# Moving a per-channel bias, a normalization and a residual shift between engines in a four-layer transformer kernel

## The chip, the cores and the metric

The kernel runs on one core of a Trainium2 chip. The metric is the device time of one execution in microseconds (us). The core has five engines that work side by side: TensorE (PE, with its weight loads as PEld), VectorE (DVE), ScalarE (ACT), GpSimd (POOL) and SyncE (SP, which only issues DMAs here). Each has its own queue of instructions, in order; between engines there are semaphores.

## The reference

32 sequences of 256 tokens with 128 channels go through four layers, each an attention-like and a feed-forward part with pre-normalization and a residual. The change touches three places.

The end of layer 0's attention-like part (a gated long convolution):

```
u, v, g = split(xn @ in_w + in_b)
y   = the state-space scan of silu(conv(u))
out = (y * sigmoid(g) + silu(v)) @ out_w + out_b
x   = x + out
```

Layer 3's mixer, a scan over time, where x is the normalized residual:

```
shifted = x moved one token later, a zero in front
inp = mix * x + (1.0 - mix) * shifted
h   = relu(inp @ W_in.T + b_in)
state = state * decay + h_t                            # over the 256 tokens
out = states @ W_out.T + b_out;   x = x + out
```

The very end: layer 3's feed-forward holds an attention, a mixture of 8 experts and a last normalization with gain `g2` and shift `ln2_b`; its result is added to the residual, so the shift can be added to the residual at any earlier time.

## The kernel before, in words

The residual `x_res` lies in SBUF for the whole kernel as 64 tiles of 128 tokens x 128 channels. A stage of this kind is a block in which each engine runs its own program over 16 units of 4 tiles (512 tokens). Stages are separated by barriers, and between them `stats` turns the collected `bn_stats` into mean and 1/deviation. A helper `staggered(engine, units, slots, (lag, work), ...)` writes a software pipeline: in step s it does, in the order listed, each piece of work for unit s - lag; the middle of it is a hardware loop. `sig.now(n, k)` is a wait for the k-th count of unit n, `sig.last(n, k)` for that of unit n-1, `sig.ago(n, k, m)` for that of unit n-m. `link` makes DVE wait for its own instruction.

Second stage of layer 0 ("c" in the names). Per step DVE does: normalize unit s (4 `tensor_scalar` of 128x128, helper line 411), add the projected output of unit s-3 to the residual (line 803) and take its `bn_stats` (line 345), then for unit s-1 and each of two channel blocks three 128x512 operations: `sv = (ps_v + bias) * sv` (line 790, one source in PSUM), `sg = sg * yT` (line 792) and `sv = sv + sg` (line 796), both with two sources in SBUF. PE projects unit s-1 (lines 831 and 832, into one PSUM buffer per block), turns unit s, projects unit s-2 out (line 841). ACT does the sigmoids of unit s-1 (lines 859, 861), moves the turned unit s out of PSUM (852), then scales the residual of unit s-1 (line 869, signal `c_grown`). POOL adds `out_b` to the residual, one 128x512 `tensor_tensor` per unit with both sources in SBUF (line 816); before it, POOL waits for `c_grown` of unit n and, while there is a unit n+2, for the normalization of unit n+2.

Mixer stage of layer 3 ("s"). ACT normalizes (line 2880, 4 activations per unit, three buffers `s_nrm`), PE turns, ACT copies `(1 - mix)` times the turned unit to `s_old` (line 2887), DVE mixes in one operation that reads the other part from PSUM (line 2815), PE projects, ACT applies the relu (2893), DVE scans (line 2822, two per unit), PE projects out (2861), DVE adds to the residual (2829) and takes the statistics. DVE's order in a step is add (lag 5), mix (lag 1), scan (lag 3). POOL adds `b_out` (line 2840) as soon as a unit is normalized.

Second attention ("h3"). After each sequence's attention, DVE adds the result to `x2`, takes `bn_stats` of it, and adds `b2` (the last shift) to two tiles of `x_res` (line 2400, 128x256). Then the router, and `sorted_experts`: DVE computes places, POOL issues 64 indirect DMAs that scatter the rows (line 1634) while DVE computes four small results more (lines 1553 to 1559).

Of the kernel before, what the change touches and what calls it, by code (L numbers as in the profile page):

```python
# [12 lines left out]
ACT = mybir.ActivationFunctionType  # L13
# [161 lines left out]
def build(nc, x_in, pack_in, maskb_in, w0_in, w1_in, w3_in, out, ktab, ychan, q_stack, k_stack, ones_rows, v_ones,  # L175
          m_parts, xs1, xs3, ys):
    ctx = ExitStack()
    with ctx:
# [132 lines left out]
        s_in, s_pr, s_re, s_sc, s_o, s_x = (sig("s_mixed", 1), sig("s_proj", 1), sig("s_relu", 1),  # L311
# [438 lines left out]
        with ExitStack() as st:  # L750
# [12 lines left out]
            with pool.loop_block(NU) as block:  # L763
# [760 lines left out]
        def sorted_experts(tag, sel, weight, src, xs, w, w_in, f_dim, func, normed=None, rows=None):  # L1524
# [13 lines left out]
            with ExitStack() as st:  # L1538
# [723 lines left out]
        def attend(tag, causal, dst, w, buffers, load, shifted=None):  # L2262
# [15 lines left out]
            with ExitStack() as st:  # L2278
# [40 lines left out]
                with pool.loop_block(NB) as block:  # L2319
# [21 lines left out]
                    def _(dve):  # L2341
# [44 lines left out]
                        def step(b, u, r, first, turn, body, tail):  # L2386
# [399 lines left out]
        with ExitStack() as st:  # L2786
            S = 3
            nrm = [sb(f"s_nrm{j}", [P, UT, P], stack=st) for j in range(S)]
            old = [sb(f"s_old{j}", [P, 2, SEQ + 1], stack=st) for j in range(S)]
            shift = sb("s_shift", [P, NT], stack=st)  # L2790
# [5 lines left out]
            ps_t = bank("s_ps_t", st, S)  # L2796
            ps_h = bank("s_ps_h", st, 2)
            ps_o = bank("s_ps_o", st, S)
            with pool.loop_block(NU) as block:
                k_set = n_chain[0] + 4 + S  # L2800

                @block.vector
                def _(dve):
                    for j in range(S):
                        link(dve, dve.memset(old[j][:, :, :], 0.0))
                    link(dve, dve.scalar_tensor_tensor(shift[:, :], mean[:, :], -1.0, rstd[:, :], ALU.mult, ALU.mult))
                    link(dve, dve.memset(dec[:, :], 1.0))
                    link(dve, dve.tensor_scalar(dec[:, :], dec[:, :], c("decay"), None, ALU.mult))
                    link(dve, dve.tensor_scalar(omix[:, :], c("mix"), -1.0, 1.0, ALU.mult, ALU.add))

                    def mix(n, j, r):
# [3 lines left out]
                        dve.scalar_tensor_tensor(mixed[j][:, :, :], ps_t[:, j, :].rearrange("p (b t) -> p b t", b=2), c("mix"),  # L2815
                                                 old[j][:, :, 0:SEQ], ALU.mult, ALU.add).then_inc(s_in.sem, 1)
# [16 lines left out]
                    staggered(dve, NU, S, (5, added), (1, mix), (3, scan))  # L2833
# [12 lines left out]
                def _(pe):  # L2846
                    def turn(n, j, r):
                        turn_tiles(pe, fr_s.tps, ps_t[:, j, :], nrm[j], UT, fr_s.nrm.now(n, 1), s_in.ago(n, 1, S))

                    def project(n, j, r, h):  # L2850
                        pe.wait_ge(*s_in.now(n, 1))
                        pe.wait_ge(*s_re.ago(n, 1, 2))
                        pe.matmul(ps_h[:, h, :], c("win3"), mixed[j][:, :, :].rearrange("p b t -> p (b t)"),
# [11 lines left out]
                    for n in range(NU + 4):  # L2865
                        if 0 <= n - 2 < NU:
                            project(n - 2, (n - 2) % S, (n - 2) // S, (n - 2) % 2)
                        if n < NU:
                            turn(n, n % S, n // S)
                        if 0 <= n - 4:  # L2870
                            project_out(n - 4, (n - 4) % S, (n - 4) // S)
# [256 lines left out]
```

## Time and profile before

| | |
|---|---|
| time, median of 3 runs | 3247.86 us (3245.29 to 3249.93) |
| time of the profiled execution | 3245.29 us |
| its span in the profile | 3243.2 us |
| TensorE clock granted, mean | 0.91 of full speed |
| busy in the span | PE 2553.1 us (79%), DVE 2129.7 (66%), ACT 1631.4 (50%), POOL 764.2 (24%) |
| second stage of layer 0 | from 271 to 393.5 us |
| mixer stage of layer 3 | from 2274.8 to 2345.0 us |
| second attention | from about 2480 to 2911.8 us |
| scatter before the last experts | from 2980 to 3061.5 us |

Shares are averages over many stages with different limits. The kernel is a chain of stages with barriers, so a stage's length is what counts, and in it the engine that is busy without a gap. The 2.1 us between the profiled time and its span lie outside the instructions.

### The profile page before, as it was taken

The numbers are of one execution on the slowest core, as the hardware profiler recorded it, in microseconds if no ns is written. First come the engines' busy times: TensorE is split into PE (matmuls) and PEld (weight loads), VectorE is DVE, ScalarE is ACT, GpSimd is POOL, SyncE is SP. The second block draws the span as 40 slices with busy tenths as digits, with TensorE's granted clock in tenths as the row PEclk, the third lists the DMA queues.
The fourth block names the chain that finished last, engine by engine and source line by source line (L and its number), as shares of the span: only waits on it lengthen the run. The fifth ranks groups of instructions, "written<-read, shape, count | busy, mean of one in ns | idle before, by whom it ended". The sixth has DMA issues, their size and how long they took to land. (4 is left out here: it accounts for less than half of the span.)

```text
span 3243.2 us, 69838 instructions
## 1 busy us (share of the span) xinstructions
PE 2553.1 (79%) x20225; PEld 1822.0 (56%) x20225; DVE 2129.7 (66%) x4755; ACT 1631.4 (50%) x3623; POOL 764.2 (24%) x1097
## 2 busy tenths in 40 slices
PE   4657859989988786999459999997676999984191
PEld 2334543449877533999237777767443666653180
DVE  5967875237778633777756666657876888855086
ACT  1646513332254443667535666652553777764063
POOL 0000100000000176555432222200251222211670
PEclk7889979999999898999779999998888999997595
DMA  3095100111190211222594566500086566521133
GB/s 104 0 213 143 46 13 20 35 43 49 36 172 0 78 53 51 71 69 67 171 243 53 72 72 70 69 6 1 1 263 68 72 72 72 72 25 45 52 100 111
DMA packets 316152, 241.10 MB, mean 74 GB/s; under 512 B 27069, under 2 KB 297837, under 8 KB 315693
## 3 DMA queue, kind: packets, MB, share of 16 engines
q1 hardware_dynamic: 288248, 202.91, 31.6%
q0 software_dynamic: 19072, 28.28, 3.0%
q10 hardware_dynamic: 8704, 8.39, 0.9%
q8 instruction: 58, 0.95, 0.1%
q14 instruction: 70, 0.57, 0.1%
HBM read 139.83 MB, written 96.51 MB: 73 GB/s over the span
## 5 line engine op out<-in xcount | busy, mean ns | idle before, releaser
L2619 ACT ACTIVATE h_pt<-h_ps 128x384 f32<-128x384 f32 (+1 forms) x1024 | 543.5, 545 | 278.1 <-PE h_ps L2528 143.5
L2365 DVE TENSOR_REDUCE h_nm<-h_ps 128x4 f32<-128x1024 f32 (+1 forms) x448 | 539.2, 1218 | 153.9 <-PE h_ps L2499 62.3
L1900 POOL DMA_INDIRECT results<-e_y,e_ykey x208 | 217.0, 1043 | 162.6 <-DVE e_y L1889 143.5
L1857 DVE TENSOR_SCALAR e_wt<-w 128x1156 f32 (+1 forms) x208 | 141.2, 680 | 166.1 <-PEq L1626 87.7
L2547 PE MATMUL h_ps_o<-h_pt,h_vp 128*32 128x256 f32 (+1 forms) x4096 | 246.8, 358 | 1.3 <-ACT h_pt L2619 1.3
L1947 ACT ACTIVATE e_hid<-e_ps_h,e_wt 128x128 f32<-128x128 f32 x688 | 201.3, 369 | 13.4 <-PE e_ps_h L1921 8.8
L2533 PE MATMUL h_ps<-h_sq,h_sk 128*128 128x256 bf16 x1024 | 193.4, 275 | 9.2 <-ACT h_pt L2619 4.3
L1929 PE MATMUL e_ps_o<-e_wt,e_hid 128*128 128x128 f32 x1376 | 192.4, 279 | 4.8 <-DVE e_y L1889 4.8
L1921 PE MATMUL e_ps_h<-e_hT,e_wt 128*128 128x128 f32 x1376 | 195.1, 281 | 0.6 <-ACT e_hT L1942 0.3
L2470 PE MATMUL h_ps<-h_sk,h_sq 128*128 128x256 bf16 x1024 | 156.1, 276 | 42.6 <-DVE h_identb L2347 36.6
L1704 POOL DMA_INDIRECT sorted_rows<-e_row,e_pos x128 | 124.6, 974 | 256.2 <-DVE e_row L1682 218.3
L1921 PEld LDWEIGHTS e_ps_h<-e_hT,e_wt 128*128 128x128 f32 x1376 | 172.3, 194 | 9.0 <-issue 3.2
L1929 PEld LDWEIGHTS e_ps_o<-e_wt,e_hid 128*128 128x128 f32 x1376 | 170.7, 192 | 8.1 <-DVE e_y L1889 8.0
L1942 ACT ACTIVATE e_hT<-e_ps_t 128x128 f32<-128x128 f32 x208 | 57.6, 278 | 217.7 <-PE e_ps_t L1914 211.3
L2547 PEld LDWEIGHTS h_ps_o<-h_pt,h_vp 128*32 128x32 f32 x4096 | 106.8, 109 | 92.5 <-issue 36.7
L2414 POOL TENSOR_TENSOR h_mpart<-h_nm,h_zero 128x32 bf16<-128x32 f32 x64 | 15.0, 234 | 580.5 <-DVE h_nm L2365 580.5
L1914 PE MATMUL e_ps_t<-pack,e_xt 128*128 128x128 f32 x208 | 57.5, 278 | 110.2 <-DMA e_xt<-sorted_rows 110.0
L2525 PE MATMUL h_ps<-h_sq,h_sk 128*128 128x256 bf16 x512 | 140.4, 274 | 2.1 <-ACT h_pt L2619 1.7
L349 PE MATMUL stats_ps_d<-pack 128*128 128x384 f32 x136 | 65.9, 654 | 96.7 <-PEq L166 86.3
L2528 PE MATMUL h_ps<-h_mskb 128*128 128x256 bf16 x512 | 139.6, 273 | 0.0
L1223 DVE TENSOR_TENSOR x_hid<-x_gelu,x_ps_u 128x512 f32<-128x512 f32 x64 | 43.3, 686 | 142.3 <-ACT x_gelu L1208 142.3
L2470 PEld LDWEIGHTS h_ps<-h_sk,h_sq 128*128 128x128 bf16 x1024 | 99.7, 99 | 59.1 <-DVE h_identb L2347 36.8
(457 smaller groups left out, 6249.7 us busy)
## 6 DMA issues: line engine op xcount, KB each, us to landing
h_sk<-k_stack SPq DMA_DIRECT2D x192, 128.0 KB
q_stack<-p_parts SPq DMA_DIRECT2D x64, 256.0 KB, 3.0
h_sq<-q_stack SPq DMA_DIRECT2D x64, 256.0 KB
sorted_rows<-pad SPq DMA_DIRECT2D x26, 520.0 KB, 10.6
e_xt<-sorted_rows SPq DMA_DIRECT2D x104, 130.0 KB, 2.2
e_got<-results SPq DMA_DIRECT2D x24, 512.0 KB, 4.7
k_stack<-p_parts SPq DMA_DIRECT2D x32, 384.0 KB, 3.0
b_tz<-ktab SPq DMA_DIRECT2D x32, 256.0 KB, 7.1
```

The source lines that it names most:

```text
L1857: dve.tensor_scalar(wt[j % 4][:, :], w[:, :, :].rearrange("p e w -> p (e w)")[:, ds(at, wc)], 1.0, None, ALU.mult).then_inc(e_w.sem, 1)
L1900: gp.indirect_dma_start(ys[:, :], bass.IndirectOffsetOnAxis(ap=key[m // 4][:, m % 4:m % 4 + 1], axis=0), y[m][:, :], None).then_inc(return ...
L1921: pe.matmul(ps_h[:, k, 0:P], wt[j % 4][:, f * P:(f + 1) * P], hT[j % 4][:, :], start=True, stop=True).then_inc(e_h.sem, 1)
L1929: ins = pe.matmul(o, hid_t[m][:, f, :], wt[m][:, f_dim + f * D:f_dim + (f + 1) * D], start=(f == 0), stop=(f == nf - 1))
L1947: act.activation(hid_t[j % 4][:, f, :], ps_h[:, (j * nf + f) % 4, 0:P], func, bias=wt[j % 4][:, o_b1 + f:o_b1 + f + 1]).then_inc(e_a.sem, 1)
L2365: dve.tensor_reduce(to, got, AX, ALU.max, negate=True).then_inc(s["mx"].sem, 1)
L2470: ins = pe.matmul(ps_1[:, h % 4, q * SEQ:(q + 1) * SEQ], sq[u][:, h, q * P:(q + 1) * P], sk[u][:, h, :], start=True, stop=True)
L2525: pe.matmul(o[:, 0:SEQ], sk[u][:, hd, 0:P], sq[u][:, hd, :], start=True, stop=False, skip_group_check=True)
L2528: ins = pe.matmul(o.rearrange("p (t q) -> p t q", q=SEQ)[:, :, 0:P], mskb[:, 0:P], mskb[:, 2 * P:3 * P].unsqueeze(1).to_broadcast([P, 2, P ...
L2533: ins = pe.matmul(o[:, t * SEQ:(t + 1) * SEQ], sk[u][:, hd, t * P:(t + 1) * P], sq[u][:, hd, :], start=True, stop=True)
L2547: ins = pe.matmul(ps_o[32 * j:32 * (j + 1), q0:], vp[u % 2][:, t, head(HG * g + j), :], pt[g % 2][:, j, t * SEQ:(t + 1) * SEQ - q0], start ...
L2619: act.activation(pt[g % 2][:, j, :], ps_2[:, h % 2, 0:SW], ACT.Exp, scale=scale).then_inc(s["ex"].sem, 1)
```

## The change

Three things are rewritten.

1. Stage c: POOL no longer waits for the normalization of unit n+2 before it adds `out_b`, and its program becomes a `staggered` loop. PE's projection of a block waits until DVE has finished the previous unit's last operation on that block (`c_z`, line 796), where it waited for the first (`c_v`, line 790).
2. Stage s: the normalization goes from ACT to DVE (helper line 411) with one buffer `s_nrm` in place of three; ACT copies the turned unit unscaled to `s_hT`; the mix becomes two DVE operations, both from SBUF; PSUM buffers for the turned and the projected unit go from 3 and 2 to 1 each; DVE's order becomes normalize (lag 0), add (4), scan (2), mix (1).
3. The 32 adds of `b2` inside the second attention go, and one 128x8192 add stands behind DVE's small results in the scatter block.

```diff
@@ stage c, POOL
                         gp.wait_ge(*c_grown.now(n, 1))
-                        if not isinstance(n, int) or n + 2 < NU:
-                            gp.wait_ge(*fr_c.nrm.now(n + 2, 1))
...
-                    for n in range(NU):
-                        biased(n, n % S, n // S)
+                    staggered(gp, NU, S, (0, biased))
@@ stage c, PE
                         for b in range(CB):
-                            pe.wait_ge(*c_v.last(n, b + 1))
+                            pe.wait_ge(*c_z.last(n, b + 1))
@@ stage s, buffers
-            nrm = [sb(f"s_nrm{j}", [P, UT, P], stack=st) for j in range(S)]
-            old = [sb(f"s_old{j}", [P, 2, SEQ + 1], stack=st) for j in range(S)]
-            shift = sb("s_shift", [P, NT], stack=st)
+            nrm = sb("s_nrm", [P, UT, P], stack=st)
+            hT = [sb(f"s_hT{j}", [P, 2, SEQ + 1], stack=st) for j in range(S)]
...
-            ps_t = bank("s_ps_t", st, S)
-            ps_h = bank("s_ps_h", st, 2)
+            ps_t = bank("s_ps_t", st)
+            ps_h = bank("s_ps_h", st)
@@ stage s, DVE
+                    def normed(n, j, r):
+                        norm_tiles(dve, fr_s.nrm, nrm, x_res, n * UT, UT, rstd, fr_s.tps.last(n, 1))
...
-                        dve.scalar_tensor_tensor(mixed[j][:, :, :], ps_t[:, j, :].rearrange("p (b t) -> p b t", b=2), c("mix"),
-                                                 old[j][:, :, 0:SEQ], ALU.mult, ALU.add).then_inc(s_in.sem, 1)
+                        dve.tensor_scalar(mixed[j][:, :, :], hT[j][:, :, 0:SEQ], omix[:, :], None, ALU.mult
+                                          ).then_inc(s_in0.sem, 1)
+                        dve.wait_ge(*s_in0.now(n, 1))
+                        dve.scalar_tensor_tensor(mixed[j][:, :, :], hT[j][:, :, 1:], c("mix"), mixed[j][:, :, :],
+                                                 ALU.mult, ALU.add).then_inc(s_in.sem, 1)
...
-                    staggered(dve, NU, S, (5, added), (1, mix), (3, scan))
+                    staggered(dve, NU, S, (0, normed), (4, added), (2, scan), (1, mix))
@@ stage s, PE
-                    for n in range(NU + 4):
...
+                    staggered(pe, NU, S, (2, project), (0, turn), (3, project_out))
@@ stage s, ACT
-                    def normed(n, j, r):
...
-                        act.activation(old[j][:, :, 1:], ps_t[:, j, :].rearrange("p (b t) -> p b t", b=2), ACT.Copy,
-                                       scale=omix[:, :]).then_inc(fr_s.hT.sem, 1)
+                        act.activation(hT[j][:, :, 1:], ps_t[:, 0, :].rearrange("p (b t) -> p b t", b=2), ACT.Copy
+                                       ).then_inc(fr_s.hT.sem, 1)
...
-                    for n in range(NU + 3):
-                        for lag, work in ((3, positive), (0, normed), (1, older)):
+                    staggered(act, NU, S, (2, positive), (0, turned))
@@ second attention, DVE
-                                if shifted is not None:
-                                    x_last = x_res[:, ds((b - 1) * TPB, TPB), :]
-                                    dve.tensor_tensor(x_last, x_last, shifted.unsqueeze(1).to_broadcast([P, TPB, D]), ALU.add)
@@ scatter block, DVE
                             places(dve)
+                            beside(dve)
...
+                def residual_shifted(dve):
+                    link(dve, dve.tensor_tensor(x_res[:, :, :], x_res[:, :, :], c("b2").unsqueeze(1).to_broadcast([P, NT, D]),
+                                                ALU.add))
```

On PE at the start of stage c, the instructions stand as they did; what a projection (`c_ps_v`) waits for is another signal. `signal32` is DVE's `c_v`, `signal33` its `c_z`, `signal38` ACT's moved unit `c_hT`. Before:

```order
L420 MATMUL c_ps_t<-pack,c_nrm 128x128 x3
L831 MATMUL c_ps_v<-c_hT,pack 128x512 [waits signal32,signal38]
L832 MATMUL c_ps_g<-c_hT,pack 128x512
L831 MATMUL c_ps_v<-c_hT,pack 128x512 [waits signal32]
L420 MATMUL c_ps_t<-pack,c_nrm 128x128 [waits signal38,signal30]
```

Now:

```order
L420 MATMUL c_ps_t<-pack,c_nrm 128x128 x3
L828 MATMUL c_ps_v<-c_hT,pack 128x512 [waits signal33,signal38]
L829 MATMUL c_ps_g<-c_hT,pack 128x512
L828 MATMUL c_ps_v<-c_hT,pack 128x512 [waits signal33]
L420 MATMUL c_ps_t<-pack,c_nrm 128x128 [waits signal38,signal30]
```

Each pair of projections moved behind two more DVE operations of the unit ahead of it; the turning of the next unit stands behind them in PE's queue as it did.

On DVE at the start of stage s, from the memsets to the second scan (`s_mix` is the mixed input, `s_state` the scan's result, `s_rel` the relu's). Before:

```order
L2805 MEMSET s_old 128x514 x3
L2806 SCALAR_TENSOR_TENSOR s_shift<-mean,rstd 128x64
L2807 MEMSET s_dec 128x256
L2808 TENSOR_SCALAR s_dec<-s_dec,pack 128x256
L2809 TENSOR_SCALAR s_omix<-pack 128x1
L2815 SCALAR_TENSOR_TENSOR s_mix<-s_ps_t,pack,s_old 128x512 x3
L2822 SCALAR_TENSOR_TENSOR s_state<-s_dec,s_rel 128x256 x2
```

Now:

```order
L2799 MEMSET s_hT 128x514 x3
L2800 MEMSET s_dec 128x256
L2801 TENSOR_SCALAR s_dec<-s_dec,pack 128x256
L2802 TENSOR_SCALAR s_omix<-pack 128x1
L411 TENSOR_SCALAR s_nrm<-x_res,mean,rstd 128x128 x8
L2811 TENSOR_SCALAR s_mix<-s_hT,s_omix 128x512
L2814 SCALAR_TENSOR_TENSOR s_mix<-s_hT,pack,s_mix 128x512
L411 TENSOR_SCALAR s_nrm<-x_res,mean,rstd 128x128 x4
L2821 SCALAR_TENSOR_TENSOR s_state<-s_dec,s_rel 128x256 x2
```

Four small operations and a second mixing operation per unit came to DVE, and a unit is scanned one step after it is mixed, where two steps lay between.

On DVE in the scatter block, where `e_past` to `e_place` are the small results and the next block begins with the loads of `e_place`. Before:

```order
L1553 TENSOR_TENSOR e_past<-pack,e_tend 128x504
L1557 TENSOR_REDUCE e_placef<-e_past 128x72
L1558 TENSOR_SCALAR e_placef<-e_placef 128x72
L1559 CAST e_place<-e_placef 128x72
L1626 UNCONDITIONAL_BRANCH
```

Now:

```order
L1550 TENSOR_TENSOR e_past<-pack,e_tend 128x504
L1554 TENSOR_REDUCE e_placef<-e_past 128x72
L1555 TENSOR_SCALAR e_placef<-e_placef 128x72
L1556 CAST e_place<-e_placef 128x72
L2937 TENSOR_TENSOR x_res<-x_res,pack 128x8192
L1623 UNCONDITIONAL_BRANCH
```

The add of 64 tiles stands last in the block, behind everything that another engine needs from DVE there.

## Rows read from the trace of the kernel before

**Rows 1.** Windows: stretch, length, busy PE PEld DVE ACT POOL, PEclk, DMA share, GB/s.

```profile
292.00:330.00 38.00, 34.88 (x163) 20.53 (x162) 35.49 (x83) 29.37 (x54) 7.67 (x6) 1.00 0.25 81
2289.00:2327.00 38.00, 27.40 (x138) 19.05 (x138) 36.62 (x80) 27.82 (x61) 14.17 (x10) 0.91 0.00 1
2500.00:2910.00 410.00, 399.10 (x4161) 252.62 (x4160) 326.52 (x473) 298.33 (x602) 96.67 (x261) 1.00 0.53 64
```

**Rows 2.** Timeline: start, us, engine, line, operation; DVE over one unit, second stage.

```profile
326.22 1.11 DVE L411 TENSOR_SCALAR c_nrm<-x_res,mean,rstd 128x128 f32 x4
327.24 0.68 DVE L803 TENSOR_TENSOR x_res<-x_res,c_ps_o 128x512 f32 x1
...
328.99 0.73 DVE L790 SCALAR_TENSOR_TENSOR c_sv<-c_ps_v,pack,c_sv 128x512 f32<-128x512 f32 x1
...
331.69 0.68 DVE L792 TENSOR_TENSOR c_sg<-c_sg,c_yT 128x512 f32<-128x512 f32 x1
332.48 0.69 DVE L796 TENSOR_TENSOR c_sv<-c_sv,c_sg 128x512 f32<-128x512 f32 x1
333.21 1.11 DVE L411 TENSOR_SCALAR c_nrm<-x_res,mean,rstd 128x128 f32 x4
```

**Rows 3.** Timeline: PE, ACT and POOL around the same unit.

```profile
324.96 1.13 PE L831 MATMUL c_ps_v<-c_hT,pack 128*128 128x512 f32 x2
...
326.98 0.69 ACT L859 ACTIVATE c_sv<-c_ps_v,pack 128x512 f32<-128x512 f32 x1 [0.70 <-PE c_ps_g L832]
...
327.47 1.28 POOL L816 TENSOR_TENSOR x_res<-x_res,spread 128x512 f32<-128x512 f32 x1 [5.70 <-DVE c_nrm L411]
...
328.85 1.64 ACT L869 ACTIVATE x_res<-x_res,c_sink,c_grow  x4
```

**Rows 4.** Timeline: DVE and POOL at the same stage's end, POOL not waiting for DVE.

```profile
378.82 0.69 DVE L796 TENSOR_TENSOR c_sv<-c_sv,c_sg 128x512 f32<-128x512 f32 x1
...
379.20 1.44 POOL L816 TENSOR_TENSOR x_res<-x_res,spread 128x512 f32<-128x512 f32 x1 [1.82 <-ACT x_res L869]
...
380.09 1.10 DVE L792 TENSOR_TENSOR c_sg<-c_sg,c_yT 128x512 f32<-128x512 f32 x1
```

**Rows 5.** Timeline: DVE and ACT in the scan stage.

```profile
2289.77 0.99 DVE L345 BATCH_NORM_STATS2 bn<-x_res  x4
...
2326.90 2.30 DVE L2822 TENSOR_TENSOR_SCAN s_state<-s_dec,s_rel 128x256 f32<-128x256 f32 x2
...
2329.81 0.87 DVE L345 BATCH_NORM_STATS2 bn<-x_res 128x6 f32<-128x128 f32 x4
...
2331.25 1.27 DVE L2822 TENSOR_TENSOR_SCAN s_state<-s_dec,s_rel 128x256 f32<-128x256 f32 x2
...
2332.55 0.69 ACT L2893 ACTIVATE s_rel<-s_ps_h,pack 128x512 f32<-128x512 f32 x1 [3.08 <-PE s_ps_h L2853]
```

**Rows 6.** Groups by line: names, shapes, count, busy us, mean ns, idle before.

```profile
L590 DVE TENSOR_SCALAR a_cv<-a_up,pack 128x512 f32<-128x512 f32 x32 | 15.9, 539 | 0.0
...
L1396 DVE TENSOR_SCALAR l_low<-l_qk 128x512 f32<-128x512 f32 x32 | 13.7, 427 | 1.1
```

**Rows 7.** Timeline: first and last work of the scan stage.

```profile
2274.75 1.65 ACT L2880 ACTIVATE s_nrm<-x_res,s_shift,rstd 128x128 f32<-128x128 f32 x4 [5.42 <-DVE s_omix L2809]
...
2344.11 0.87 DVE L345 BATCH_NORM_STATS2 bn<-x_res 128x6 f32<-128x128 f32 x4
```

**Rows 8.** Group and timeline: the add of b2, end of the second attention.

```profile
L2400 DVE TENSOR_TENSOR x_res<-x_res,pack 128x256 f32 (+1 forms) x32 | 13.0, 407 | 0.0
...
2911.36 0.41 DVE L2400 TENSOR_TENSOR x_res<-x_res,pack 128x256 f32<-128x256 f32 x1
```

**Rows 9.** Timeline: DVE beside POOL's indirect DMAs, and DVE after the last scatter.

```profile
1126.09 0.97 POOL L1704 DMA_INDIRECT sorted_rows<-e_row,e_pos  x1 [0.30 <-issue]
1126.27 1.14 DVE L1553 TENSOR_TENSOR e_past<-pack,e_tend 128x952 f32<-128x952 f32 x1
...
3069.22 0.98 DVE L1857 TENSOR_SCALAR e_wt<-w 128x642 f32 x2 [87.74 <-PEq L1626]
```

More of the change, by code:

```diff
@@ L1519, in _, with sorted_experts @@
                     staggered(act, NB, S, (2, gated), (0, keep), (2, powers))
-        def sorted_experts(tag, sel, weight, src, xs, w, w_in, f_dim, func, normed=None, rows=None):
+        def sorted_experts(tag, sel, weight, src, xs, w, w_in, f_dim, func, normed=None, rows=None, beside=None):
             choices = len(sel)
@@ L2260, in build, with attend @@
         BLOCKS = GROUPS // 2
-        def attend(tag, causal, dst, w, buffers, load, shifted=None):
+        def attend(tag, causal, dst, w, buffers, load):
             s = attns[tag]
@@ L2804, in _ @@
                     for j in range(S):
-                        link(dve, dve.memset(old[j][:, :, :], 0.0))
-                    link(dve, dve.scalar_tensor_tensor(shift[:, :], mean[:, :], -1.0, rstd[:, :], ALU.mult, ALU.mult))
+                        link(dve, dve.memset(hT[j][:, :, :], 0.0))
                     link(dve, dve.memset(dec[:, :], 1.0))
@@ L2847, in turn, with project @@
                     def turn(n, j, r):
-                        turn_tiles(pe, fr_s.tps, ps_t[:, j, :], nrm[j], UT, fr_s.nrm.now(n, 1), s_in.ago(n, 1, S))
-                    def project(n, j, r, h):
+                        turn_tiles(pe, fr_s.tps, ps_t[:, 0, :], nrm, UT, fr_s.nrm.now(n, 1), fr_s.hT.last(n, 1))
+                    def project(n, j, r):
                         pe.wait_ge(*s_in.now(n, 1))
-                        pe.wait_ge(*s_re.ago(n, 1, 2))
-                        pe.matmul(ps_h[:, h, :], c("win3"), mixed[j][:, :, :].rearrange("p b t -> p (b t)"),
+                        pe.wait_ge(*s_re.last(n, 1))
+                        pe.matmul(ps_h[:, 0, :], c("win3"), mixed[j][:, :, :].rearrange("p b t -> p (b t)"),
                                   start=True, stop=True).then_inc(s_pr.sem, 1)
@@ L2875, in _, with turned @@
                     act.wait_ge(chained, k_set)
-                    def normed(n, j, r):
-                        act.wait_ge(*fr_s.tps.ago(n, 1, S))
-                        for t in range(UT):
-                            ins = act.activation(nrm[j][:, t, :], x_res[:, n * UT + t, :], ACT.Identity,
-                                                 scale=rstd[:, n * UT + t:n * UT + t + 1], bias=shift[:, n * UT + t:n * UT + t + 1])
-                        ins.then_inc(fr_s.nrm.sem, 1)
-                    def older(n, j, r):
+                    def turned(n, j, r):
                         act.wait_ge(*fr_s.tps.now(n, 1))
                         act.wait_ge(*s_in.ago(n, 1, S))
-                        act.activation(old[j][:, :, 1:], ps_t[:, j, :].rearrange("p (b t) -> p b t", b=2), ACT.Copy,
-                                       scale=omix[:, :]).then_inc(fr_s.hT.sem, 1)
+                        act.activation(hT[j][:, :, 1:], ps_t[:, 0, :].rearrange("p (b t) -> p b t", b=2), ACT.Copy
+                                       ).then_inc(fr_s.hT.sem, 1)
                     def positive(n, j, r):
@@ L2892, in positive @@
                         act.wait_ge(*s_sc.ago(n, 2, S))
-                        act.activation(rel[j][:, :, :], ps_h[:, n % 2, :].rearrange("p (b t) -> p b t", b=2), ACT.Relu,
+                        act.activation(rel[j][:, :, :], ps_h[:, 0, :].rearrange("p (b t) -> p b t", b=2), ACT.Relu,
                                        bias=c("bin3")).then_inc(s_re.sem, 1)
-                    for n in range(NU + 3):
-                        for lag, work in ((3, positive), (0, normed), (1, older)):
-                            if 0 <= n - lag < NU:
-                                work(n - lag, (n - lag) % S, (n - lag) // S)
+                    staggered(act, NU, S, (2, positive), (0, turned))
         stats(x_res)
@@ L2907, in build @@
                                       bv=every_row("bv3")), heads_in, load_heads, keep=(x2, every_row("bo3")))
[L2908 removed]
+            attend("h3", False, x2, dict(o=c("wo3")), heads_in, load_heads)
             stats(x2)
@@ L2951, in build @@
                 stl.close()
-                sorted_experts("e3", (chosen[:, :, :],), (gp[:, :],), x2, xs3, w, w3_in, F3, ACT.Relu, rows=x2_rows)
+                def residual_shifted(dve):
+                    link(dve, dve.tensor_tensor(x_res[:, :, :], x_res[:, :, :], c("b2").unsqueeze(1).to_broadcast([P, NT, D]),
+                                                ALU.add))
+                sorted_experts("e3", (chosen[:, :, :],), (gp[:, :],), x2, xs3, w, w3_in, F3, ACT.Relu, rows=x2_rows,
+                               beside=residual_shifted)
             collect("e3", 1, x2)
```

11 lines of the change are left out of this document (2 added, 9 removed).

## The prediction

> **What bounds the kernel now.** I read the stage windows first, then the timeline of one unit in each changed stage, then the edges of the stages. The windows [rows 1] give the limit of each: in 38 us of stage c DVE is busy for 35.49, in 38 us of stage s for 36.62, and in 410 us of the second attention PE is busy for 399.10 and DVE only for 326.52. So the two first stages last as long as DVE's queue, and what the change adds there is paid in full; the attention lasts as long as PE's queue, and what it takes from DVE there is not. The unit in stage c [rows 2] shows it again: normalizations start at 326.22 and 333.21, 6.99 apart, and DVE's records follow each other all the way.
>
> **Stage c.** DVE's own operations stay. What changes is when POOL adds `out_b`. Before, POOL waits for the normalization and runs at 327.47 [rows 3], beside DVE's add that reads PSUM, which keeps its 0.68 us [rows 2]; nobody loses. Without the wait POOL starts when ACT has scaled the residual. What then happens is seen where the kernel before has no unit n+2 to wait for [rows 4]: POOL starts at 379.20 while DVE's SBUF-SBUF add (378.82 to 379.51) still runs, takes 1.44 in place of 1.28 and ends at 380.64, 1.13 after that add; the next DVE operation with two SBUF sources starts at 380.09 and takes 1.10 in place of 0.68, ending 0.55 after POOL. So POOL's add and such a DVE operation exclude each other. The Trainium skill (SBUF — State Buffer, "Who interferes with whom") has the rule: a VectorE instruction with two SBUF inputs contends with a GpSimd instruction that reads SBUF, and whoever is first holds the port for its whole instruction. By that rule every collision costs the later engine what is left of the earlier one's instruction, and the trace agrees, with its 0.42 us; were the port shared by halves, the loss would be half of the overlap, 0.28 for the 0.55 that line 792 spends beside POOL.
>
> Where does POOL land now? Offsets are from DVE's normalization at 326.22. PE may start block 1's projection only after the last operation of the unit before on that block, which ends at about 0.0 (333.17 for the next step), so at 0.1; before, it started at 324.96, that is -1.26. ACT's first sigmoid of that block comes 2.02 after PE's start, and ACT's scaling of the residual 1.87 after that sigmoid, behind a second sigmoid and the move of the turned unit (326.98 and 328.85, [rows 3]): 2.1 and 4.0. The scaling's 1.64 ends at 5.6, where it ended at 4.3. Nothing in DVE waits for this: the two sigmoids (0.69 each) are done by 3.5, and block 1's first DVE operation stands just ahead of line 792, at 4.8. POOL asks at 5.7 to 5.8. DVE's line 792 holds 5.47 to 6.15 [rows 2], so POOL's add ends 1.13 later, at 7.28, and line 796, which would start at 6.26, ends 0.55 after that at 7.83 in place of 6.95: +0.88. In units where ACT's scaling comes a little later, POOL finds line 796 in its place, ends at 8.1 and holds the next normalization: +1.1. I take 0.9 for 16 units, 14.4, less three stalls of about 0.42 that the kernel before already has at the stage's first and last units [rows 4], 1.3. PE's later start costs something in the first unit or two, when nothing is buffered; at most the two operations it now waits for, 0.69 + 0.69 [rows 2]; I take 1. Stage c: 14.4 - 1.3 + 1.0 = **+14.1**. Bounds: only one 0.42 per unit, as in [rows 4], makes +5.4; 1.1 each and 1.4 at the start make +17.7.
>
> **Stage s.** Before, ten units take from 2289.77 to 2329.81 [rows 5], 4.00 each. After, I add up DVE's queue per step. Normalization, add and statistics are the same sequence as in stage c, and the operation behind them starts 2.77 after the normalization (328.99 - 326.22, [rows 2]); I use that for the scans' start. Two scans take 1.27 [rows 5] and the next operation starts 0.09 before they end (as 327.24 against 326.22 + 1.11 in [rows 2]): 1.18. The mix is now two operations. No row has the first one, a 128x512 `tensor_scalar` with one pointer scalar: [rows 6] has 0.427 with none and 0.539 with two, so it lies between and I take 0.48. The second waits for it (0.10, as line 796 behind line 792: 332.48 - 332.37 in [rows 2]) and is priced as line 790, a `scalar_tensor_tensor` of that size, 0.73. Mix: 0.48 + 0.10 + 0.73 - 0.09 = 1.22. Step: 2.77 + 1.18 + 1.22 = **5.17**, against 4.00.
>
> Does anything make it longer? The scan needs the relu. It ends 2.0 us after the mix before it (2331.25 is the mix's end less 0.08, the relu ends at 2333.24, [rows 5]), and 2.77 of other DVE work lies between. At half clock two projections take about 1 us more, and the relu would end at 3.0: a wait of 0.2 in such a step. POOL's add starts 0.14 to 0.2 behind the normalization (327.47 against 327.33, [rows 2, 3]), so it lasts from 1.3 to 2.6, beside the add that reads PSUM and the statistics, and is out just before the scans at 2.77. Before, some scan pairs collided with it, 2.30 for 1.27 [rows 5]; that loss is inside the 4.00. If POOL's add lasted into the scans it would cost up to 1.0 per step.
>
> The new order has 12 full steps (4 to 15) in its loop: 12 x 5.17 = 62.0. The four filling steps run on latency: with one `s_nrm`, the second normalization waits until PE has turned the first; then mix, projection, relu and scan one after another. From DVE's records and PE at half clock I get 5.5 for steps 0 and 1, 5.3 for step 2 and 4.8 for step 3, 15.6. The four draining steps: 4.7 (add, statistics, a wait for the relu, scans, mix), 3.4, 1.75 and 1.75, 11.6. Start: 2274.75 less the small operation that is gone, 2274.4 [rows 7]. End: 2274.4 + 15.6 + 62.0 + 11.6 = 2363.6, against 2344.11 + 0.87 = 2344.98 [rows 7]. Stage s: **+18.6**. Bounds: +15 if the first mix is at 0.43, the fill at 14 and the drain at 10; +25 if the relu or POOL's add costs 0.5 in each full step. ACT loses 64 activations, which cost nothing and save nothing.
>
> **Second attention.** Gone are 32 adds of 0.407 [rows 8], 13.0 of DVE. They lie beside PE, whose idle time is 11 us of 410 [rows 1]. Only the last has nothing to hide it: it is the stage's last work, 2911.36 [rows 8]. **-0.4**; bounds 0 and -11.
>
> **Scatter block.** The new add has 8192 columns. [rows 9]: 952 columns take 1.14; with 512 in 0.69 [rows 2] a column costs 1.02 ns, so 8192 take 8.6 us. It is hidden: DVE is idle for 87.74 before its next block while POOL scatters [rows 9]. POOL's indirect DMAs must not be held by it; the one row of such a DVE operation beside them has POOL at its 0.97 and DVE at its 1.14 [rows 9]. **0**, at worst +8.6. The Trainium skill warns, in DMA: Bandwidth & Descriptors ("SWDGE vs HWDGE vs iDMA"), that GpSimd writes its descriptors through the SBUF access from which VectorE's 2-port modes lock it out; SBUF — State Buffer, "Who interferes with whom", adds that `tensor_tensor` takes only the read side and did not stall them. If the add locked POOL out, the block would be up to 8.6 longer, by the second sentence nothing; the one row that the trace has agrees with the second.
>
> **Sum.** 14.1 + 18.6 - 0.4 + 0 = +32.3. The profiled execution took 3245.29, so 3277.6; it is the fastest of the three runs, and on their median 3247.86 I get 3280.2. I predict **3280**.
>
> **Rivals.**
> - *The collision in stage c is cheap.* POOL's request falls just behind a DVE operation that reads PSUM, and each unit pays the 0.42 of [rows 4], stage c +5.4: 3271. For it: that is the only price seen in steady rows. Against: there PE's projection was 1.26 earlier.
> - *Both stages lose their margin.* In c 1.1 per unit, in s 0.5 per step from POOL's add or a half-clock PE: 17.7 + 25 - 0.4 = +42: 3290. For it: the margins in s are 0.1 to 0.2 us.
> - *The big add stops POOL's scatter,* +8.6: 3289. POOL's next indirect DMA would wait for DVE's whole instruction. Against it stands [rows 9]; for it, that this row covers 1.1 us and not 8.6.
> - *The attention was paced by DVE after all, and the kernel is not slower.* PE's ends are modelled, and its 399.10 busy of 410 [rows 1] may hide waits for maxima behind the adds. The removal must then shorten each of 32 sequences by 32.7 / 32 = 1.02 us, 2.5 times the operation removed, to bring the time to 3248 or less; from there the kernel is not slower. Taking just the operations' own 13.0 gives 3268. Against: DVE is idle for 83 of the 410 us there.
> - *The change doesn't do what it says* in c: POOL's wait gone moves nothing, since ACT's scaling comes as late as the normalization. Then c is +1 and the time 3267. Against: POOL asks at 5.8, and the old wait ended at 8.1 (6.99 + 1.11, [rows 2]).
>
> **Chances.** Forecast (3275 to 3286) 0.58; cheap collision 0.13; margins lost 0.12; scatter held 0.06; POOL unmoved 0.07; attention paced by DVE 0.04, of which half reaches no change. Range: 3266 to 3292; it leaves out the far ends of both sides. A measurement can tell about 0.2% from no change, 6.5 us: faster 0.01, same 0.02, slower 0.97.
>
> **What would show it.** In stage c: line 796 of block 1 (or the normalization behind it) at 1.5 us and more where it was 0.69, POOL's add starting inside DVE's line 792, and normalizations 7.9 apart. In s: starts of normalization 5.2 apart, no idle time on DVE in the full steps, scans at 1.27 a pair, the first mix at 0.48, the stage about 89 us long. In the attention the same length to a microsecond, with DVE 13 less busy. In the scatter block an add of 8.6 us and indirect DMAs at 0.97 throughout. I am wrong if the units of c stay 7.0 apart, if those of s come nearer to 4 than to 5, or if the attention gets shorter by more than 2 us.

## The result

The changed kernel takes 3276.06 us (median of 4 runs, 3275.61 to 3285.74), the kernel before beside it 3246.57 us (median of 4, 3245.17 to 3249.93): a ratio of 1.0096, 95% interval 1.0084 to 1.0108. It is slower by 0.96%; the forecast was 3280 in a range of 3266 to 3292, and "slower" had 0.97. The profiled execution of the changed kernel has a span of 3278.0 us against 3243.2, so the profiles have 34.8 us to explain, for which the prediction had 32.3.

The sum is near, but its parts are not all right. Each stage ends in a short stretch of statistics whose first record (line 361 of both kernels) cuts the span into stretches that can be compared:

| stretch | before us | after us | difference | predicted |
|---|---|---|---|---|
| start to the end of stage c | 393.75 | 403.55 | +9.8 | +14.1 |
| five unchanged stretches to the start of stage s | 1873.24 | 1872.87 | -0.4 | 0 |
| stage s | 78.30 | 98.46 | **+20.2** | +18.6 |
| projections and second attention | 566.78 | 564.95 | -1.8 | -0.4 |
| scatter block, experts, collection | 293.60 | 301.78 | **+8.2** | 0 |
| the rest | 37.55 | 36.39 | -1.2 | 0 |

The start holds an unrelated +1.0 (first statistics at 52.3 and 53.3) and -1.5 up to stage c's first normalization (271.11 and 270.61); from that normalization to its statistics stage c takes 122.64 before and 132.95 after, **+10.3**. Unchanged stretches differ by 1 us and more between executions (567.90 and 566.69, 108.80 and 109.77), so neither -1.8 nor -1.2 needs a cause.

The windows that answer to [rows 1] (same columns), the middle one over the longer stage s:

```profile
292.00:330.00 38.00, 29.88 (x140) 18.07 (x139) 35.82 (x73) 26.21 (x47) 6.76 (x6) 1.00 0.21 68
...
2284.00:2374.00 90.00, 55.40 (x224) 36.51 (x224) 80.22 (x206) 20.21 (x32) 20.38 (x16) 0.79 0.00 0
...
2529.00:2939.00 410.00, 398.65 (x4155) 252.12 (x4152) 318.45 (x442) 297.55 (x601) 91.69 (x261) 1.00 0.53 64
```

In stage c DVE is as full as before (35.82 of 38) with 73 instructions where it did 83: same busy share, less work. In the attention DVE lost 8 us of busy time in this window (the prediction's sign was 13) and PE did not change.

**Stage c after.** The timeline of DVE, ACT and POOL over one unit (start, duration, engine, line; in brackets the engine's idle time before it and what ended it):

```profile
339.46 1.10 DVE L411 TENSOR_SCALAR c_nrm<-x_res,mean,rstd 128x128 f32 x4
...
343.43 1.64 ACT L866 ACTIVATE x_res<-x_res,c_sink,c_grow  x4
...
344.96 0.68 DVE L792 TENSOR_TENSOR c_sg<-c_sg,c_yT 128x512 f32<-128x512 f32 x1
345.27 1.49 POOL L814 TENSOR_TENSOR x_res<-x_res,spread 128x512 f32 x1 [6.28 <-ACT x_res L866]
345.74 1.57 DVE L796 TENSOR_TENSOR c_sv<-c_sv,c_sg 128x512 f32<-128x512 f32 x1
...
347.23 1.10 DVE L411 TENSOR_SCALAR c_nrm<-x_res,mean,rstd 128x128 f32 x4
```

Read against [rows 2]: normalizations are 7.77 apart, not 6.99. ACT's scaling ends at 345.07, POOL starts 5.81 after the normalization, inside line 792 (344.96 to 345.64), and ends at 346.76; line 796 ends 0.55 later at 347.31, as the chain in the prediction had it, with 1.57 us where [rows 2] has 0.69. The groups of DVE in the stage (count, then busy us and mean ns of one) say what that comes to, the kernel after:

```profile
L796 DVE TENSOR_TENSOR c_sv<-c_sv,c_sg 128x512 f32<-128x512 f32 x32 | 32.9, 1027 | 3.3
...
L792 DVE TENSOR_TENSOR c_sg<-c_sg,c_yT 128x512 f32<-128x512 f32 x32 | 23.5, 734 | 0.0
L411 DVE TENSOR_SCALAR c_nrm<-x_res,mean,rstd 128x128 f32 (+1 forms) x64 | 18.8, 353 | 1.2 <-PE c_ps_t L420 1.2
```

and before:

```profile
L792 DVE TENSOR_TENSOR c_sg<-c_sg,c_yT 128x512 f32<-128x512 f32 x32 | 23.1, 723 | 0.0
L796 DVE TENSOR_TENSOR c_sv<-c_sv,c_sg 128x512 f32<-128x512 f32 x32 | 22.1, 692 | 3.3
L411 DVE TENSOR_SCALAR c_nrm<-x_res,mean,rstd 128x128 f32 (+1 forms) x64 | 17.8, 341 | 1.4 <-PE c_ps_t L420 1.2
```

The mean of 1027 hides two values, 0.69 and 1.57. That is 10.8 + 0.4 + 1.0 = 12.2 us more of DVE for the same work, some of it in the filling units, where DVE waits anyway. A line of 796 with a mean of 1027 ns and no wait in front of it is what this contention looks like in a profile: it is counted as busy time of the operation and never as idle time.

**Stage s after.** DVE, PE, ACT and POOL over one full step:

```profile
2326.49 1.11 DVE L411 TENSOR_SCALAR s_nrm<-x_res,mean,rstd 128x128 f32 x4
2326.71 2.07 PE L2852 MATMUL s_ps_h<-s_mix,pack 128*128 128x512 f32 x2 [2.52 <-DVE s_mix L2814]
2327.52 0.68 DVE L2828 TENSOR_TENSOR x_res<-x_res,s_ps_o 128x512 f32 x1
2327.80 1.26 POOL L2839 TENSOR_TENSOR x_res<-x_res,spread 128x512 f32 x1 [3.82 <-DVE s_nrm L411]
2328.34 0.98 DVE L345 BATCH_NORM_STATS2 bn<-x_res  x4
...
2328.91 0.69 ACT L2879 ACTIVATE s_rel<-s_ps_h,pack 128x512 f32<-128x512 f32 x1 [4.91 <-PE s_ps_h L2852]
...
2329.63 1.28 DVE L2821 TENSOR_TENSOR_SCAN s_state<-s_dec,s_rel 128x256 f32<-128x256 f32 x2 [0.30 <-ACT s_rel L2879]
...
2330.82 0.46 DVE L2811 TENSOR_SCALAR s_mix<-s_hT,s_omix 128x512 f32<-128x512 f32 x1
2331.32 0.75 DVE L2814 SCALAR_TENSOR_TENSOR s_mix<-s_hT,pack,s_mix 128x512 f32<-128x512 f32 x1
```

Every duration of the step's sum is there: scans at 1.28 a pair (none at 2.30 as in [rows 5]), the first mix at 0.46 (taken: 0.48), the second at 0.75 (0.73). The starts of the twelve full steps are 5.2 apart on average. This step is the longest of them, 5.55: PE's two projections took 2.07 where others take 1.12 (granted clock 0.50 of full speed from 2326.7 to 2328.8, 0.99 in the 5 us before), so the relu came late and the scans waited 0.30. The prediction had put 0.2 on that. In these full steps POOL's add meets no long record of DVE; in the filling ones it meets two, a normalization (four from 2285.91 take 1.45 for 1.11) and a second mix (1.64 at 2287.80 for 0.75).

**The scatter block after.** DVE and POOL:

```profile
3004.86 0.68 DVE L1550 TENSOR_TENSOR e_past<-pack,e_tend 128x504 f32<-128x504 f32 x1 [0.88 <-PEq L1571]
3005.15 1.30 POOL L1632 DMA_INDIRECT sorted_rows<-x,e_pos  x1 [90.94 <-PEq L1623]
...
3006.75 8.73 DVE L2937 TENSOR_TENSOR x_res<-x_res,pack 128x8192 f32<-128x8192 f32 x1
3006.76 0.99 POOL L1632 DMA_INDIRECT sorted_rows<-x,e_pos  x1 [0.30 <-issue]
3008.06 8.27 POOL L1632 DMA_INDIRECT sorted_rows<-x,e_pos  x1 [0.30 <-issue]
3016.63 0.97 POOL L1632 DMA_INDIRECT sorted_rows<-x,e_pos  x1 [0.30 <-issue]
```

One indirect DMA takes 8.27 us, from 3008.06 to 3016.33: it ends 0.85 after DVE's add (3015.48). The 64 scatters take 7.6 us longer, first start to last (80.4 before, 87.9 after). That is the rival with 0.06 in the prediction, and it came true. The two POOL rows above the long one matter too. The DMA that starts together with the add has 0.99 and is not stalled; the first one, which starts inside a 504-column `tensor_tensor`, has 1.30 (in the kernel before the first one starts 0.01 after that `tensor_tensor` has ended, and has 1.04).

### The profile page after: what moved, and what is told of

The parts are those of the page before. It is cut to its first block and busy times, and to the rows that moved or that the text cites. A ratio compares the mean times of both kernels' runs of the same rounds, so it can differ in the third digit from the quotient of the medians.

```text
span 3278.0 us, 70059 instructions
## 1 busy us (share of the span) xinstructions
PE 2556.2 (78%) x20225; PEld 1825.7 (56%) x20225; DVE 2164.3 (66%) x4803; ACT 1606.8 (49%) x3559; POOL 769.1 (23%) x1097
```

## The experiments

The kernel before ran at 3277, 3290 and 3245 us in the three sets of runs below: the level differs from set to set, mostly by the two expert stages (the stretch between the fourth and the fifth statistics took 541 us in the first profile, 539 in the last set and 557 to 567 in the two between, in kernels that leave it untouched). So a ratio is taken only against the kernel before of its own set, and stage lengths come from each run's own profile. Stages c and s are nearly free of that (c 121.7 to 123.6, the stretch of s 77.8 to 79.9, in all kernels that do not touch them). The five runs from PE's wait alone to POOL's later add in stage s are one execution each: they are read by the lengths of their stages and not by their total.

**The three parts alone.** First stage c, all its edits, on the kernel before (POOL's loop becomes a `staggered` one as well; not shown here):

```
-                        if not isinstance(n, int) or n + 2 < NU:
-                            gp.wait_ge(*fr_c.nrm.now(n + 2, 1))
-                            pe.wait_ge(*c_v.last(n, b + 1))
+                            pe.wait_ge(*c_z.last(n, b + 1))
```

> The kernel before with the edits of stage c alone: POOL's out_b add no longer waits for the normalization two units later, and PE's projection waits for the last add of the unit before on its block (c_z) instead of its first operation (c_v). Theory (the SBUF access is held for a whole instruction; POOL's add lands inside line 792 of block 1 and line 796 behind it waits): stage c +10.3 us as in the changed kernel (from the first normalization to the statistics 122.6 before, 133.0 after), twelve steady units at 7.9 instead of 7.0, line 796 of block 1 at 1.57; total +9 to +11. Rival (the collisions of stage c are an effect of the whole changed program, such as where its other stages leave the clock): stage c within 2 us of before.

Measured: ratio 1.0039 (1.0025 to 1.0053), +12.8 us by that ratio (9 to 11 were expected); stage c 132.87, +10.2; line 796 of block 1 at 1.57 to 1.61 in eleven consecutive units. As the theory has it, and independent of the other parts: from the second on, the normalizations are as far apart as in the changed kernel to 0.01 us.

The edits of stage s alone (all of that stage's part of the diff):

> The kernel before with the edits of stage s alone. Theory: DVE's queue sets the step, 5.2 us in twelve full steps; stage s (first normalization to the end of its last statistics) 90.5 in place of 70.2, total +19 to +21. Rival (part of the stage's loss in the changed kernel comes from a lower clock handed on by stage c or the tail): under +17.

Measured: ratio 1.0057 (1.0040 to 1.0074), +18.7 us, just under the 19 to 21 that were expected; the stretch of stage s 98.07 us, against 98.46 in the changed kernel and 78.30 before. The loss is there without the other parts. From the first normalization to the end of the last statistics it is 88.7 us, against 90.7 in the changed kernel and 70.2 before; the remaining 1.3 us or so of the stretch lie ahead of the first normalization, which comes 9.05 after the statistics' first record (7.49 in the changed kernel, and 9.31 in the next run, whose stage s is the old one).

The move of the `b2` adds alone (32 adds out of the attention, one beside the scatter):

> The kernel before with the adds of b2 moved alone: the 32 of the second attention gone, one 128x8192 add beside POOL's scatter. Theory (a tensor_tensor of two SBUF sources holds back POOL's indirect DMA for its whole length): one indirect DMA of about 8.3 us, the stretch from the attention's statistics to the last statistics 8 us longer, the attention 0.4 to 2 shorter; total +6 to +8. Rival (the 8 us of the changed kernel's scatter block come from elsewhere, such as slower transfers behind it): indirect DMAs at 0.97 and total -2 to 0.

Measured: ratio 1.0028 (1.0010 to 1.0046), +9 us, the expected 6 to 8 being well inside the interval. The profile of this kernel, DVE and POOL in the scatter block:

```profile
2998.80 8.76 DVE L2952 TENSOR_TENSOR x_res<-x_res,pack 128x8192 f32<-128x8192 f32 x1
2998.84 0.99 POOL L1635 DMA_INDIRECT sorted_rows<-x,e_pos  x1 [0.30 <-issue]
3000.13 8.27 POOL L1635 DMA_INDIRECT sorted_rows<-x,e_pos  x1 [0.30 <-issue]
3008.71 0.97 POOL L1635 DMA_INDIRECT sorted_rows<-x,e_pos  x1 [0.30 <-issue]
```

The same 8.27, the scatters again 87.6 from first to last. The attention's stretch took 564.87, inside the 562.5 to 568.6 of all kernels, with and without these adds: its gain cannot be told from nothing (seven kernels with the adds have a mean of 565.7, five without them 564.4).

The three ratios add up to +1.24%, with an uncertainty of about 0.28%, against +0.96% for the whole change: too coarse to show whether the parts are independent. The profiles' lengths are finer: 10.2 in stage c, 19.8 in the stretch of stage s and 7.3 in the scatters, 37.3 together, against 10.3, 20.2 and 7.6 in the changed kernel.

**Which edit of stage c costs.** POOL's wait removed (again with the `staggered` loop) and PE's wait as it was:

```
-                        if not isinstance(n, int) or n + 2 < NU:
-                            gp.wait_ge(*fr_c.nrm.now(n + 2, 1))
```

> The kernel before with POOL's wait in stage c gone and nothing else; PE's projection still waits for c_v. Theory: ACT's scaling then ends 4.3 after the normalization and POOL asks at 4.45, while line 796 of block 0 (4.20 to 4.89) holds the access; POOL ends near 6.1 and line 792 of block 1, due at 5.47, ends 0.42 late. So +0.42 in each of some 12 units, line 792 at 1.10 and not 796 at 1.57: stage c +5 us, units at 7.4. Rival (the removed wait alone makes the whole loss, PE's later start adds nothing): +10.3, line 796 at 1.57. Second rival (nothing collides because ACT is late anyway): 0.

Measured: ratio 1.0023 (1.0013 to 1.0033), +7.5 us by the runs, stage c 129.43 by the profile, +6.8. Its timeline in a steady unit:

```profile
326.81 1.60 POOL L814 TENSOR_TENSOR x_res<-x_res,spread 128x512 f32 x1 [5.80 <-ACT x_res L866]
...
327.20 0.74 DVE L790 SCALAR_TENSOR_TENSOR c_sv<-c_ps_v,pack,c_sv 128x512 f32<-128x512 f32 x1
327.87 1.10 DVE L792 TENSOR_TENSOR c_sg<-c_sg,c_yT 128x512 f32<-128x512 f32 x1
```

POOL's record starts inside line 796 of block 0, and line 792 of block 1 has 1.10 in 13 units, twelve of them consecutive; line 796 of block 1 is back at 0.69. That is the prediction's "cheap collision" (0.42 a unit, [rows 4]), as the order of the two engines makes it. The 6.8 exceeds 12 x 0.42 = 5.0: in the stage's first units POOL also holds line 796 three times, at 1.76 or 1.77.

PE's wait alone, POOL's wait kept:

```
-                            pe.wait_ge(*c_v.last(n, b + 1))
+                            pe.wait_ge(*c_z.last(n, b + 1))
```

> The kernel before with PE's projection waiting for c_z instead of c_v, and POOL's wait for the normalization kept. Theory: PE's later start alone costs DVE nothing in steady units, since the sigmoids are done by 3.5 of the unit and DVE wants them at 4.8; POOL still runs beside the add that reads PSUM: units at 7.0, stage c 122.6 to 124 (at most 1.4 more in its first units). Rival (PE's start is a loss of its own and only seems to act through POOL): units above 7.3.

Measured: stage c 122.11 us, a little less than before. So PE's later start is free by itself. It costs only together with the other edit: it moves POOL's add from 4.53 to 5.81 after the normalization, from a place where a collision costs 0.42 to one where it costs 0.88. The same profile shows this once more: its 15th unit, for which POOL never had the wait, has line 796 at 1.57, where the kernel before has line 792 at 1.10 in that unit. The removed wait makes 6.8 of the 10.2 us and PE's later start turns that into 10.2; what each costs is set by the phase between POOL and DVE.

**What stage s pays for.** The new order, with DVE normalizing, but the mix again one operation that reads PSUM and ACT's scaled copy (against the changed kernel, lines shortened):

```
-  dve.tensor_scalar(mixed[j], hT[j][:, :, 0:SEQ], omix, None, ALU.mult)
-  dve.scalar_tensor_tensor(mixed[j], hT[j][:, :, 1:], c("mix"), mixed[j], ALU.mult, ALU.add)
+  dve.scalar_tensor_tensor(mixed[j], ps_t[:, j, :], c("mix"), old[j][:, :, 0:SEQ], ALU.mult, ALU.add)
```

> The kernel before with stage s as in the changed kernel but for the mix: DVE normalizes, in the new order, and the mix is again one scalar_tensor_tensor that reads PSUM and ACT's scaled copy. Splits the stage's loss. Theory (sum of DVE's queue): a full step is 5.17 - 0.48 - 0.10 = 4.6, so the stretch between the statistics around stage s is 98.3 - 16 x 0.58 = 89, against 78.3 of before: two thirds of the loss is the smaller, one third... that is, 9.3 of 20 are the second mix operation and 11 are the normalization on DVE. Rival (the new order with one nrm tile and one projection bank sets a latency of its own): full steps above 4.9.

Measured: the stretch of stage s 87.98 us. Its DVE queue, one step:

```profile
2313.86 1.10 DVE L411 TENSOR_SCALAR s_nrm<-x_res,mean,rstd 128x128 f32 x4
2314.89 0.68 DVE L2830 TENSOR_TENSOR x_res<-x_res,s_ps_o 128x512 f32 x1
2315.71 0.98 DVE L345 BATCH_NORM_STATS2 bn<-x_res  x4
2316.61 1.25 DVE L2823 TENSOR_TENSOR_SCAN s_state<-s_dec,s_rel 128x256 f32<-128x256 f32 x2
2317.79 0.72 DVE L2816 SCALAR_TENSOR_TENSOR s_mix<-s_ps_t,pack,s_old 128x512 f32<-128x512 f32 x1
2318.43 1.11 DVE L411 TENSOR_SCALAR s_nrm<-x_res,mean,rstd 128x128 f32 x4
```

4.57 a step, nearly without a gap, where 4.6 was summed. So of 20.2 us the second mix operation is 98.46 - 87.98 = 10.5, and the normalization on DVE with its new order the other 9.7. The latter is less than 16 x 1.02 = 16.3. The new order also ends the collisions of POOL with the scans (all at 0.69 or less here), and the run on POOL's wait in stage s, below, prices those at 5.9; 16.3 - 5.9 = 10.4 is near 9.7, but that this is the whole difference is argued and not shown.

**What holds the indirect DMA.** `b2`'s row is first copied to a PSUM bank; the add of 8192 columns then has one source in SBUF (against the changed kernel, lines shortened):

```
+    link(dve, dve.tensor_copy(b2_ps[:, 0, 0:D], c("b2")))
-    ... x_res, x_res, c("b2").unsqueeze(1) ...
+    ... x_res, x_res, b2_ps[:, 0, 0:D].unsqueeze(1) ...
```

> The kernel before with the adds of b2 moved beside the scatter as in the changed kernel, but b2's row is first copied to PSUM, so that the 128x8192 add has one SBUF source. Theory (what holds POOL is a DVE instruction with two SBUF sources): the add takes about 8.7 us and every indirect DMA beside it 0.97 to 1.05; from the first to the last start of the 64 scatters 80.3. Rival (a long DVE instruction holds POOL whatever it reads): one indirect DMA of 8.3 us, 87.6 again.

Measured:

```profile
2996.76 8.69 DVE L2956 TENSOR_TENSOR x_res<-x_res,e_ps_b 128x8192 f32<-128x8192 f32 x1
2997.77 0.97 POOL L1638 DMA_INDIRECT sorted_rows<-x,e_pos  x1 [0.30 <-issue]
2999.04 0.97 POOL L1638 DMA_INDIRECT sorted_rows<-x,e_pos  x1 [0.30 <-issue]
```

The add lasts as long as before, 8.69, and the DMAs beside it take 0.97 (the first, at its start, 0.99); the scatters are at 80.3. For this add one operand's place decides. The other way to give the access up is shorter instructions, 16 adds of 512 columns with both sources in SBUF:

> The kernel before with the adds of b2 moved beside the scatter, cut into 16 adds of 128x512, two SBUF sources each. Theory (the access is held for one instruction and then given up): an indirect DMA waits only for what is left of one add of 0.69, so some eight of them at 1.0 to 1.7 us, 64 scatters in 82 to 84. Rival (DVE's next add takes the access before POOL gets it): one indirect DMA of 8 us or more, as with the single add.

Measured:

```profile
3004.06 9.79 DVE L2954 TENSOR_TENSOR x_res<-x_res,pack 128x512 f32<-128x512 f32 x16
3004.10 0.99 POOL L1635 DMA_INDIRECT sorted_rows<-x,e_pos  x1 [0.31 <-issue]
3005.39 1.48 POOL L1635 DMA_INDIRECT sorted_rows<-x,e_pos  x1 [0.30 <-issue]
3007.17 1.50 POOL L1635 DMA_INDIRECT sorted_rows<-x,e_pos  x1 [0.30 <-issue]
```

Five DMAs (some eight were expected) wait about 0.53 each, 2.6 in all; the scatters take 82.9, inside the 82 to 84. POOL gets in between two adds, so the hold is for one instruction and DVE's queue does not starve it. It is more than the half of 0.69 that a chance arrival would wait; the DMAs have fallen into step with the adds: they start 1.81 apart, three adds of 0.60, and each just after an add has started.

**The other way round.** The kernel before has such collisions too: seven of its 32 scans meet POOL's add (a pair of them in [rows 5], 2.30). If what costs is one engine holding the other for a whole instruction, POOL's wait is to be moved and not removed:

```
                     def biased(n, j, r):
-                        gp.wait_ge(*fr_s.nrm.now(n, 1))
+                        gp.wait_ge(*s_sc.now(n, 2))
```

> The kernel before with one edit in stage s: POOL's add of bout3 waits for the scans of its own unit instead of its normalization, so that it runs beside DVE's add that reads PSUM and the statistics. Theory: no scan pair meets POOL any more, all at 1.27 or less; the seven scans that were long lose 4.9 us together (sum 25.3 to 20.3), and stage s is 3 to 5 us shorter (78.3 between the statistics around it, to 73.5 to 75.5). Rival (latency between ACT, PE and DVE takes the time back, since the scans came early for nothing): under 1.5 shorter.

Measured, in stage s:

```profile
2294.41 1.26 DVE L2822 TENSOR_TENSOR_SCAN s_state<-s_dec,s_rel 128x256 f32<-128x256 f32 x2
...
2295.59 0.66 DVE L2829 TENSOR_TENSOR x_res<-x_res,s_ps_o 128x512 f32 x1
...
2295.86 1.27 POOL L2840 TENSOR_TENSOR x_res<-x_res,spread 128x512 f32 x1 [2.26 <-DVE s_state L2822]
...
2296.40 0.98 DVE L345 BATCH_NORM_STATS2 bn<-x_res  x4
```

No scan above 0.685 us, POOL inside DVE's add that reads PSUM and the statistics, and steps of 3.5. The stretch of stage s is 72.45 us, 5.9 less than in the kernel before (from the first normalization to the end of the last statistics 64.4 against 70.2): more than the 3 to 5 expected, and more than the 5.0 that the seven long scans lose together. With the `b2` adds beside the scatter, their row in PSUM, as well:

> The kernel before with two edits: POOL's add in stage s waits for the scans as in the run before this one, and the adds of b2 stand beside the scatter with b2's row in PSUM. Theory: -3 to -5 in stage s, -0.4 for the last add of the attention, the scatters at 80.3 from first to last: total -4 to -6 us, a ratio of 0.998 to 0.999, at the edge of what can be told. Rival (the stage gives nothing back): 0.9995 to 1.0005.

Measured: 3239.84 us (12 runs) against 3244.64 (17 runs) of the kernel before, ratio 0.9985, 95% interval 0.9977 to 0.9994. Stage s 72.44, scatters 80.3. This is faster than the kernel before, if only by 4.8 us; what part of it the `b2` adds have cannot be told.

## Why the prediction was right, and where it was not

- **Bound.** That stages c and s last as long as DVE's queue held: each part's loss was there alone, and the steps followed sums of DVE's durations, 5.2 for 5.17 and 4.57 for 4.6.
- **Stage c, +14.1 predicted, +10.3 measured.** The mechanism was right, to a few hundredths of a microsecond: POOL's add starts at 5.81, line 796 ends 0.88 late. The size was off in one factor: "0.9 for 16 units". Eleven units have line 796 of block 1 at 1.57 to 1.61 and two more have line 792 held, at 1.35 and 1.75; in the filling ones some collisions (line 796 at 1.75 at 284.17) fall on a DVE that waits anyway, and the last unit has none. From the fourth normalization (291.36) to the sixteenth (386.20) twelve intervals take 94.8 us, against 83.7 (291.14 to 374.86) before: +11.1. The fill adds 0.7 (the 1.0 of the prediction), and the drain gives 1.5 back (its 1.3).
- **Stage s, +18.6 predicted, +20.2 measured.** Full steps 5.2 as summed (5.17), two of them at 5.4 and 5.55 with half-clock projections (2.01 and 2.07 a pair); fill and drain together 27.8 instead of 27.2. The term that was taken too small is PE's clock: the projections have a mean of 829 ns each in this stage, 729 before. The run with the edits of stage s alone has 732 and needs 88.7 us from its first normalization where this one needs 90.7; the prediction's sum was 89.2. Most of that 2 us lies in one filling step (5.51 against 4.79) and one draining step (4.14 against 3.19), each with half-clock projections in the longer case alone. What makes the clock differ between two executions of the same stage was not tested.
- **Second attention, -0.4 predicted.** -1.8 in this pair of profiles, but kernels that keep the adds took from 564.0 to 568.6 there and those without them 562.5 to 566.7. The adds were hidden beside PE, as [rows 1] and [rows 8] had it.
- **Scatter block, 0 predicted, +8.2 measured.** This is the step that failed, in both its halves. The row that it rested on, [rows 9], has a DMA that *started* 0.18 before the add; its 0.97 says that this add does not stop a DMA already under way, and nothing on one that asks later. The first scatter of the changed kernel (1.30 inside a 504-column add) shows the right test at the same scale. Nor was that row the only evidence in the trace of before: in the first expert stage four indirect DMAs start just after a `tensor_scalar` of DVE and take 1.50 to 1.55. The first of them:

```profile
1533.53 0.76 DVE L1857 TENSOR_SCALAR e_wt<-w 128x1156 f32 x1 [0.22 <-DVE e_y L1889]
1533.58 1.55 POOL L1900 DMA_INDIRECT results<-e_y,e_ykey  x1 [0.90 <-DVE e_y L1889]
```

  Each ends 0.84 after the `tensor_scalar`, as the DMA of 8.27 ends 0.85 after the add: DVE held POOL's DMAs before the change too, and with one SBUF source. And the same rule had been read from [rows 4] for POOL's add in stage c; it was not carried over to POOL's DMAs. The Trainium skill (SBUF — State Buffer, "Who interferes with whom") has both sentences: that a DVE instruction with two SBUF inputs contends with a GpSimd instruction that reads SBUF, which the runs with one and with two SBUF sources bear out (0.97 against 8.27), and that `tensor_tensor` did not stall DMA in a probe, on which the prediction leaned. The measurement decides for the first. That the indirect DMA is caught because it reads its row numbers from SBUF is an inference that no run here tests.
- **The total** came out 2.5 us from the sum because errors cancel, and that is luck: the sum was 3.8 too high in c, 1.4 in the attention, 1.2 in the last stretch and 0.9 in the start and the unchanged stretches, and 1.6 too low in s and 8.2 in the scatter block.

## What to carry to other kernels

Look for instructions whose duration has two values in one group: where GpSimd runs beside VectorE, the longer one can be a wait that the profile books as work, as line 796 at 0.69 and 1.57 here. Before removing a wait of GpSimd, find which VectorE operation it will then start beside; the places that cost nothing here were an add that reads PSUM and the `bn_stats`; one SBUF source alone was not enough, as the held `tensor_scalar`s show. A wait that leads to such a place can be worth more than none (5.9 us in stage s). For a long VectorE instruction beside GpSimd's DMAs, put one operand in PSUM or cut it up, and price any row as evidence only if its second engine *asked* while the first was running.

## What was not expected

- A `tensor_tensor` with two SBUF sources holds GpSimd's indirect DMA for the whole rest of its length (8.27 us beside 8.73), the same add with one source in PSUM not at all (0.97), and in 16 pieces 1.50 for each DMA met.
- The normalization, a `tensor_scalar` with one SBUF source and two pointer scalars, is held as well: in the changed kernel one of stage c takes 1.41 us at 291.61 where 0.34 is usual, beside POOL's add of 291.67 (1.27).
- A DMA under way is not safe from every DVE instruction. In the first expert stage of the kernel before, `tensor_scalar`s of 0.76 (line 1857) that start 0.36 to 0.40 after a DMA lengthen it to 1.24 to 1.28, so that it ends 0.12 after them. The two-source adds do not do this: the DMA that starts together with the add of 8.73 has 0.99, and in the run with 16 pieces the DMA of 3007.17 ends 0.84 after the one add that it waited for (3007.15, 0.68), though two more start before it ends. So the two kinds hold different parts of a DMA; which access each part needs was not tested.
- The same POOL add records 1.27 when alone and mostly 1.44 to 1.79 when DVE was first, so both sides' records contain waiting.
- Moving POOL behind the scans gained 5.9 us where the long scans had lost 5.0; the rest, the step of 3.5 against 4.0, was not taken apart.
